# Expert stage with a fifth bank of up products, one bank for both turns, and places split 10 x 128 + 1

## The reference

```python
E, K = (8, 2); capacity = int(1.25 * N * K / E) + 1      # N = 4096, so 1281
k_probs, k_idx = top_k(softmax(xf @ router_w.T), K)       # shares normalised
rank = position of the token among those of its expert; keep = rank < capacity
buf = zeros((E, capacity, H)).at[flat_e, slot].add(where(keep, xf[token_id], 0))
h = silu(einsum('ech,ehf->ecf', buf, w1))                 # H = 128, F = 512
out_buf = einsum('ecf,efh->ech', h, w2)
combined = sum over k of out_buf[flat_e, slot] * keep * k_probs
return combined + x
```

## Time and profile before

| | |
|---|---|
| median of 3 runs | 1129.29 us (1127.92 to 1129.47) |
| profiled execution, its own time | 1126.79 us |
| its span | 1125.0 us |
| TensorE busy | 993.5 us, 88% |
| VectorE busy | 832.7 us, 74% |
| ScalarE busy | 775.5 us, 69% |
| GpSimd busy | 644.6 us, 57% |
| mean granted clock of TensorE | 0.968 |

### The profile page before, as it was taken

One profiled execution on the slowest core, in us unless ns is written; L12 is line 12 of the kernel. 1 busy time (PEld: TensorE's weight loads), 2 busy tenths in 40 slices (PEclk: granted clock), 3 DMA queues, 4 the chain that ended last, 5 costly groups with the idle time before them and its releaser, 6 DMA issues. The chain is left out here.

```text
span 1125.0 us, 18399 instructions
## 1 busy us (share of the span) xinstructions
PE 993.5 (88%) x5064; PEld 426.3 (38%) x5064; DVE 832.7 (74%) x1591; ACT 775.5 (69%) x1524; POOL 644.6 (57%) x781
## 2 busy tenths in 40 slices
PE   4699999998999999869999999999999977888860
PEld 3123333333333332213344444444444354544430
DVE  4588888897888888748777767777777664565555
ACT  1067777776777777647788888888888666676651
POOL 6444545362636333336669787787878640655565
PEclk9999999999999999979999999999999998999995
DMA  2553836041314131369977886877887327112136
GB/s 58 97 89 102 186 98 131 21 81 42 59 28 71 43 48 46 105 184 272 228 206 200 236 231 182 237 208 198 227 226 205 87 89 246 54 57 78 28 99 241
DMA packets 102378, 149.78 MB, mean 133 GB/s; under 512 B 18216, under 2 KB 72088, under 8 KB 101838
## 3 DMA queue, kind: packets, MB, share of 16 engines
q1 hardware_dynamic: 95470, 139.65, 47.2%
q0 software_dynamic: 6272, 8.94, 2.8%
q10 hardware_dynamic: 544, 0.13, 0.2%
HBM read 109.44 MB, written 40.04 MB: 133 GB/s over the span
## 5 line engine op out<-in xcount | busy, mean ns | idle before, releaser
L811 ACT ACTIVATE a_probs<-a_score 128x512 f32<-128x512 f32 x512 | 291.9, 598 | 119.0 <-PE a_score L892 112.0
L987 DVE TENSOR_REDUCE a_mx<-a_mxps 128x2 f32<-128x1024 f32 x256 | 306.6, 1211 | 51.3 <-PE a_mxps L883 46.5
L1585 POOL TENSOR_TENSOR m_hidl<-m_hid,m_hidh 128x512 f16<-128x512 f32 x203 | 234.4, 1168 | 74.4 <-ACT m_hidh L1648 67.0
L1654 ACT ACTIVATE m_h<-m_h 128x512 f32<-128x512 f32 (+1 forms) x264 | 153.7, 583 | 48.7 <-PE m_h L1772 42.6
L1868 DVE TENSOR_TENSOR m_hid<-m_h,p_gates 128x512 f32<-128x512 f32 x196 | 134.0, 688 | 65.2 <-ACT m_h L1654 58.7
L904 PE MATMUL a_ops<-a_probs,a_vst 128*32 128x512 f32 x1024 | 138.1, 612 | 0.0
L1648 ACT ACTIVATE m_hidh<-m_hid 128x512 f16<-128x512 f32 x203 | 126.2, 622 | 11.0 <-DVE m_hid L1868 10.5
L1750 PE MATMUL m_y<-m_hidh,p_wdh 128*128 128x512 f16 (+1 forms) x264 | 100.3, 380 | 9.9 <-POOL m_hidl L1585 7.8
L2154 POOL DMA_INDIRECT t_picked<-e_yrow,p_rows x66 | 65.8, 998 | 75.2 <-DVE e_yrow L2289 55.6
L892 PE MATMUL a_score<-a_qstack,a_kstack 128*128 128x512 f16 x256 | 97.6, 387 | 6.7 <-ACT a_probs L811 3.5
L2302 DVE SCALAR_TENSOR_TENSOR e_hidl<-e_h,e_hidh 128x468 f16<-128x468 f32 (+1 forms) x96 | 57.5, 603 | 60.6 <-ACT e_hidh L2170 47.6
(11 more groups left out here) (308 smaller groups left out, 1933.1 us busy)
## 6 DMA issues: line engine op xcount, KB each, us to landing
p_gates<-t_cw SPq DMA_DIRECT2D x256, 256.0 KB
t_slots<-p_blank SPq DMA_DIRECT2D x8, 723.9 KB
t_qparts<-a_qparts SPq DMA_DIRECT2D x32, 128.0 KB
t_picked<-p_blank SPq DMA_DIRECT2D x8, 512.0 KB
p_raw<-up SPq DMA_DIRECT2D x8, 512.0 KB, 4.9
p_raw<-down SPq DMA_DIRECT2D x8, 512.0 KB, 5.1
p_rows<-t_slots SPq DMA_DIRECT2D x5, 723.9 KB
a_xin<-x SPq DMA_DIRECT2D x8, 256.0 KB, 5.0
```

Of the source, the lines that this page charges most:

```text
L811: act.activation(probs[:, kt % 2, g, :], score[:, g % 2, :], ACT.Exp, scale=SCALE / (QS * QS)).then_inc(exp_done, 1)
L987: dve.tensor_reduce(mx[ahead % 2][:, j // 2, g:g + 2], mxps[:, j % 2, :, :], AX.X, ALU.max).then_inc(mx_done, 1)
L1585: pool.tensor_tensor(hidl[0:r0, k % r, :], hid[0:r0, k % r, :], hidh[0:r0, k % r, :], ALU.subtract).then_inc(lo_done[0], 1)
L1654: act.activation(h, h, ACT.Silu, scale=1.0 / WS).then_inc(silu_done, 1)
```

## The change

An expert now has exactly 1281 places: MAIN = 10 x 128 in ten full tiles, and one odd place. The blocks are 4, 4 and 2 tiles; the third has one column more for the odd place: 512, 512 and 257 columns. The odd records of experts 0 to 6 are loaded together by three small DMAs (rows, shares, targets), that of expert 7 with a blank one beside it by two more; all five are issued right behind the load of expert 1. The odd result of an expert is kept as one column, and all seven are turned, scaled and scattered together with expert 6, that of expert 7 with its own.

XBANKS and XLAG go from 4 to 5. The bank for it comes from the two turns: `xps` and `ops` are now the same bank `turned`. Hence new waits: turning the rows of block B waits for the result rows of block B - 4, and turning the result of B waits for `xl_done` of B + 4 (at most all). result_out is done at f = 0 of the second block after instead of f = 3 of the next; result_turned and result_rows at f = 2 instead of f = 1; split_weights at f = 1 instead of f = 2.

```diff
-CT = 11
-CR = -(-CAPACITY // CT)
-PLACES = CT * CR
+CT = 10
+CR = P
+PLACES = CAPACITY
+MAIN = CT * CR
@@ load_places, behind the load of an expert
+    if e == ODD_WITH:
+        odd_places(sp, scratch, pre)
+ODD_LOADS, ODD_WITH = 5, 1
+def odd_places(sp, scratch, pre):
...
+    for dst, src in ((pre.odd_rows[:], odd[0:E1 - 1, 0:D]), (pre.odd_share[:], diagonal(D)), (pre.odd_to[:], diagonal(D + E1)),
+                     (pre.odd_last[0:1, :], odd[E1 - 1:E1, :]), (pre.odd_last[1:2, :], pre.blank[1:2, :])):
+        sp.dma_start(dst, src, allow_slow_non_contiguous=True).then_inc(pre.x_in[ODD_WITH], 16)
@@ blanks_out
+                    sp.dma_start(odd, pre.blank[0:E1, :]).then_inc(pre.blank_out, 16)
@@ expert phase
-BLOCKS = ((0, 4), (4, 4), (8, 3))
+BLOCKS = ((0, 4), (4, 4), (8, 2))
-XLAG = 4
-XBANKS = 4
+XLAG = 5
+XBANKS = 5
-        xps, ops = ps("x", [P, 512]), ps("o", [P, 512])
+        turned = ps("x", [P, 512])
+        xps, ops = turned, turned
+        def copied(B):
+            return B + 1 + (B + 1) // NB
+        def rowed(B):
+            return B + 1 + (B >= ALL - 1 - NB) + (B >= ALL - 1)
+        def ends(B):
+            return at(B)[1] == NB - 1 and at(B)[0] >= E1 - 2
@@ GpSimd, behind the scatters of a block
+                if ends(B):
+                    last = e == E1 - 1
...
+                    pool.indirect_dma_start(plane, bass.IndirectOffsetOnAxis(to, 0), (odd_yrow_last if last else odd_yrow)[:], None,
@@ ScalarE, result_out
+                if at(B)[1] == NB - 1:
...
+                    act.activation(one, here, ACT.Copy).then_inc(yc_done, 1)
@@ ScalarE, main loop
-                if f == 3 and B:
-                    result_out(B - 1)
+                if f == 0 and B >= 2:
+                    result_out(B - 2)
             high_part(FC * ALL - 1)
+            result_out(ALL - 2)
             result_out(ALL - 1)
@@ TensorE, rows_turned
                 if B:
                     pe.wait_ge(xl_done, B)
+                if B >= 4:
+                    pe.wait_ge(row_done, rowed(B - 4))
...
+                        op = pe.matmul(xps[:, far:far + 1], pre.odd_rows[:], ident[0:E1 - 1, e:e + 1], start=True, stop=True)
@@ TensorE, result_turned
-                pe.wait_ge(yc_done, B + 1)
+                pe.wait_ge(yc_done, copied(B))
+                pe.wait_ge(xl_done, min(B + 4, ALL))
                 if B:
-                    pe.wait_ge(row_done, B)
+                    pe.wait_ge(row_done, rowed(B - 1))
@@ TensorE, main loop
-                if f == 1 and B >= 2:
+                if f == 2 and B >= 2:
                     result_turned(B - 2)
-            result_turned(ALL - 2)
             for g in range(FC * ALL - XLAG, FC * ALL):
                 down(g)
+                if g == FC * ALL - XLAG + 2:
+                    result_turned(ALL - 2)
@@ VectorE, result_rows and main loop
+                if ends(B):
...
+                        dve.tensor_scalar(odd_yrow[:], ops[0:E1 - 1, far:far + P], pre.odd_share[:], None, ALU.mult
+                                          ).then_inc(row_done, 1)
-                if f == 2 and B in SPLIT_IN:
+                if f == 1 and B in SPLIT_IN:
                     split_weights(dve, pre, JOBS + 1 + SPLIT_IN[B])
-                if f == 1 and B >= 2:
+                if f == 2 and B >= 2:
                     result_rows(B - 2)
```

More of the change, by code:

```diff
@@ L157, in place_buffers, with odd @@
         self.rows_in = [ctx.enter_context(nc.sbuf_tensor(f"p_rows{k}", [CR, CT, REC], F32)) for k in range(XEARLY)]
+        def odd(n, p, w, dt=F32):
+            return ctx.enter_context(nc.sbuf_tensor("p_odd_" + n, [p, w], dt))
+        self.odd_rows, self.odd_share, self.odd_to = odd("rows", E1 - 1, D), odd("share", E1 - 1, 1), odd("to", E1 - 1, 1)
+        self.odd_last = odd("last", 2, REC)
         self.x_in = [ctx.enter_context(nc.semaphore(f"p_x_in{k}")) for k in range(XBUFS)]
@@ L491, in blanks_out @@
                     sp.wait_ge(pre.blank_ready, 2)
-                into = scratch["slots"][PLACES * k:PLACES * k + PLACES, :].rearrange("(p t) c -> p t c", t=CT)
+                    odd = scratch["slots"].rearrange("(e p) c -> e p c", p=PLACES)[:, MAIN, :]
+                    sp.dma_start(odd, pre.blank[0:E1, :]).then_inc(pre.blank_out, 16)
+                into = scratch["slots"][PLACES * k:PLACES * k + MAIN, :].rearrange("(p t) c -> p t c", t=CT)
                 sp.dma_start(into, pre.blank[0:CR, :].unsqueeze(1).broadcast_to([CR, CT, REC])).then_inc(pre.blank_out, 16)
@@ L2106, in cols @@
         def cols(B):
-            return slice(0, CR * at(B)[3])
+            return slice(0, CR * at(B)[3] + (at(B)[1] == NB - 1))
         def put_by(b, experts):
-            return 16 * BLOCKS[b][1] * experts
+            odd = (experts > E1 - 2) + (experts > E1 - 1) if b == NB - 1 else 0
+            return 16 * (BLOCKS[b][1] * experts + odd)
+        def copied(B):
[4 more added lines that the diff above has]
+            return at(B)[1] == NB - 1 and at(B)[0] >= E1 - 2
         def pieces(t):
@@ L2149, in _ @@
                 e, b, t0, nt = at(B)
-                pool.wait_ge(row_done, B + 1)
+                pool.wait_ge(row_done, rowed(B))
                 for t in range(nt):
@@ L2181, in result_out @@
                     act.wait_ge(o_full, B - 1)
+                if at(B)[1] == NB - 1:
+                    e, far = at(B)[0], CR * at(B)[3]
+                    one, here = odd_y[:, min(e, E1 - 2):min(e, E1 - 2) + 1], yps[:, B % 2, far:far + 1]
+                    if e == E1 - 1:
+                        one, here = odd_y_last[:], here.broadcast_to([P, 2])
+                    act.activation(one, here, ACT.Copy).then_inc(yc_done, 1)
                 act.activation(yT[B % 2][:, cols(B)], yps[:, B % 2, cols(B)], ACT.Copy).then_inc(yc_done, 1)
@@ L2282, in result_rows @@
                 rows = rows_in[e % XBUFS]
+                if ends(B):
+                    far = P * nt
+                    if e == E1 - 1:
+                        dve.scalar_tensor_tensor(odd_yrow_last[:], ops[0:2, far:far + P], pre.odd_last[:, D + e:D + e + 1],
+                                                 pre.odd_last[:, 0:D], ALU.mult, ALU.add).then_inc(row_done, 1)
+                    else:
+                        dve.tensor_scalar(odd_yrow[:], ops[0:E1 - 1, far:far + P], pre.odd_share[:], None, ALU.mult
+                                          ).then_inc(row_done, 1)
                 if e == E1 - 1:
```

27 lines of the change are left out of this document (23 added, 4 removed).

## The result

The changed kernel took 1152.28 us (median of 4 runs, 1148.91 to 1153.21), the kernel before beside it 1129.11: ratio 1.0202 [1.0181, 1.0223], 2.0% slower, +23.2 us. The forecast was 1142 with a range of 1124 to 1163; the measured time lies outside the 1134 to 1150 that the forecast itself covered, and next to the 1153 of rival 2. The profiled execution took 1148.91 us for a span of 1147.2 (before: 1126.79 and 1125.0).

The account below looks back on a forecast made before the run. The end was bound by expert 6's late result rows, 14 scatters and a tail, with TensorE idle 22.1 us behind ScalarE's holds. -25.4 + 35.1 + 1.0 + 1.4 = +12.1 on 1126.79, plus 2.5 for the median: 1142 us, range 1124 to 1163.

Parts of the forecast that it names:

- the forecast itself: The case that the changed kernel takes 1134 to 1150 us; chance 0.50.
- rival 2: Waits at block starts lower TensorE's clock: 1153 us if the seven longest do it, 1165 if most do; chance 0.13.
- The shared bank: TensorE waits for result rows at the starts of blocks 3 to 22, 1.25, 2.3 or 1.7 us each: +35.1 us.
- split_weights at f=1: Weight splitting on VectorE, moved to step 1: the same instructions beside the same cover, 0.
- ScalarE's holds: Expert stage: runs of eight scatters hold ScalarE up; they no longer form, so idle time and slow clock go, -25.4 us.
- The clock: Three half-speed stretches of TensorE in the expert stage cost 4.8 us, which go; counted within the -25.4.
- TensorE's work: Expert products over 1281 instead of 1287 columns, -0.5 us; turns plus odd column nothing within 0.3; taken as 0 in all.
- The fifth bank: Up products wait for the low half five units back, not four: 1.3 us more patience against ScalarE's holds within a block.
- The start: Five small loads on the sync queue delay the stores that the expert stage's start awaits: +1.0 us, ends 0 and 2.1.
- The tail: After the last products, still 14 scatters; GpSimd ends 13.1 us behind TensorE instead of 11.7: +1.4 us.
- The signs of a wrong forecast: TensorE's idle time ahead of the turns under 20 us in all, or ScalarE's gaps persisting with runs of four scatters.

Follow-up runs that it names:

- experiment 1: The best version: the changed kernel with a bank for each of the two turns and four up banks, without the shared bank's waits; 1105.15 us, 0.9791 to the kernel before.
- experiment 2: The changed kernel with VectorE's result rows of step 2 issued ahead of its wait for the high half; 1125.07 us, 0.9972 to the kernel before.
- Experiment 7: The changed kernel with the weights split at step 3 of the block instead of step 1; 1151.02 us, 1.0235 to the kernel before.
- experiment 8: The kernel before with the scatters of experts 0 to 6 replaced by one-column memsets, those results missing from the output; 1097.86 us, 0.9762 to the kernel before.
- experiment 4: The kernel before with only the 10 tiles of 128 rows and the odd places; banks, lag and order as before; 1122.83 us, 0.9959 to the kernel before.
- experiment 5: The kernel before, 11 tiles of 117 rows, with only the change's lag of 5 and later steps; 1123.49 us, 0.9987 to the kernel before.
- experiment 10: The kernel of experiment 1 with the weights split at step 3 instead of 1, on a second chip; 1115.09 us, 0.9922 to the kernel before.
- experiment 9: The kernel before with two GpSimd additions between the scatters of blocks 0 and 1 in experts 0 to 6, on the second chip; 1137.84 us, 1.0146.
- experiment 11: The kernel of experiment 10 with one GpSimd addition between the scatters of blocks 0 and 1 of experts 0 to 6, on a third chip; 1100.49 us, 1.0016.
- experiment 3: The changed kernel with 6, 16 or 10 unread products of 257 columns ahead of each block-start wait; 1143.2 us, 1.0123 to the kernel before.
- experiment 6: The changed kernel with four up banks instead of five, the shared bank kept and one bank unused; 1150.92 us, 1.0226 to the kernel before.
- experiment 12: The kernel of experiment 1 with one GpSimd addition between the scatters of blocks 0 and 1, on the third chip; 1100.0 us, 1.0011 to the kernel before.

## Why the prediction was right, and where it was off

It was right in sign and in both mechanisms: the stops go, the shared bank costs more. In size it was 10 to 11 us low (+12.1 forecast; +22.1 in the profiled execution, +23.2 in the medians), mostly by the clock, which belongs to rival 2.

- *The shared bank, +35.1.* Forecast 1.25, 2.3 and 1.7 us in 20 places; measured 1.26, 2.34 and 1.68 in 17 of 20 places, 38.4 in all. The excess is the three blocks with a split, at 2.97, 2.63 and 2.62 instead of 1.68. Experiments 1 and 2 show the chain behind it. That the sizes agree to 0.04 us is partly luck: from the last up product's end to the rows' end it takes 2.52 us at block 1 (2.46 worked out), but then 0.15 us pass until the turn starts (1054.27 to 1054.42), which the working left out, and the down group ends 0.16 us later behind the product than it had (1051.75 to 1052.07), which takes that off again.
- *split_weights at f=1, 0.* This step failed: the same instructions no longer have the same cover, as at f=1 they stand ahead of lo(f2) and the rows, on the chain that the change had just made the bound. +3.2. VectorE's timeline ahead of the wait of 2.97 us (TensorE's turn starts at 967.59) has the second half of a split, then the low half, then the rows:
```profile
965.29 1.22 DVE L245 SCALAR_TENSOR_TENSOR p_wdl<-p_raw,p_wdh 128x1024 f16<-128x1024 f32 x1
966.43 0.68 DVE L2378 SCALAR_TENSOR_TENSOR e_hidl<-e_h,e_hidh 128x512 f16<-128x512 f32 x1
967.03 0.41 DVE L2365 TENSOR_TENSOR e_yrow<-e_x,p_rows 128x256 f32<-128x256 f32 x1
```
  Experiment 7 adds that the other place tried, step 3, isn't free either.
- *ScalarE's holds, -25.4.* TensorE's other idle time fell by 19.8 (22.05 to 2.3), forecast 20.6. The cause was an inference from coincidence; experiment 8 confirmed it, with 27.3 us of the stage and 26.6 of the whole, the clock's part in them. That length is what matters is supported by experiments 1, 4, 5 and 10, in which six to eleven scatters close together mostly go with a stop and fours mostly parted by 1.15 us or more do not; none of these runs changes the length alone. It is not the whole rule: the last stop of experiment 1 begins four scatters into its run (the product for it ended at 1067.04) and is over at 1071.45, with seven more scatters to come, and not 1.3 us past the run's end as the prediction had it. A direct test failed (9) or fell on a chip without stops (11).
- *The clock, -4.8.* This term was mis-sized: rival 2, which I gave 0.13, came true beside the forecast. Instead of nothing, 8.6 us are lost at the low level, +3.8 over before where I had -4.8. Rival 2 put it at +11 if the seven waits of 2.3 us each did it; the low level begins behind four of the seven, and once with the wait of 2.97 us (at 967.59). The other three waits of 2.34 us were followed by no fall, so the length of a single wait doesn't decide it. The Trainium skill ("TensorE: Matmul & The Clock Gate", "A second HAM failure mode: psum-queue depth-cycling") says that short idle pieces between groups of matmuls, if frequent enough, make the clock swing between its two levels. The traces agree: the change has 20 such pieces and five low stretches behind the stage's first microseconds, and experiment 3, in which the pieces are filled and so shortened, holds a clock of 1.00 from 940 to 1100.
- *TensorE's work, 0.* 3.2 us more, of which most is this: each odd column is a matmul in two passes of its own (14 for experts 0 to 6, from 938.7 to 1076.3) and delays TensorE by 0.31 us an expert, 2.4 in all; "nothing within 0.3" was said of what comes eight times.
- *The fifth bank* was costed at 1.3 us of patience; experiment 6 shows it worth nothing here, since what it would ride out is gone or greater.
- *The start, +1.0.* The sync queue's timeline, which answers to the earlier trace rows, has the five loads where I put them, 1.9 us in all, but between the first store of t_s (918.96) and the stage's first turn (931.25) 12.29 us pass, 12.91 before: -0.6. *The tail, +1.4:* 0.9.
```profile
920.89 0.34 SPq L200 DMA_DIRECT2D p_odd_rows<-t_slots  x1
...
922.22 0.59 SPq L200 DMA_DIRECT2D p_odd_last<-p_blank  x1
923.86 0.39 SPq L1574 DMA_DIRECT2D t_s<-m_srow  x1
```

In the profiled execution: 25.7 (stage: idle 18.7, clock 3.8, work 3.2) - 0.6 + 0.9 - 0.9 (behind GpSimd's end) - 3.1 (stages ahead, where the kernels are alike, and which differ so much from run to run) = 22.0 of 22.1. The sizes of the last two are differences that these two executions show, and are not explained. The signs of a wrong forecast that I had named (idle ahead of the turns under 20 us, stops with runs of four) did not come.

What stays open is why ScalarE stops, and why only on some chips. For one that has no stops, the change should cost the shared bank in full: from 1.0202/0.9791 = 1.042 and the 1.0011 of experiment 12, about 4.3%, an estimate that no run tried.

## What to carry to other kernels

A buffer shared by two users puts the slower user's whole chain on the path at each turn; work the chain out instruction by instruction from a clean stretch (here it came to within 0.04 us) and then ask of every other moved call whether it now stands on that chain. TensorE's idle pieces of 2.3 us, repeated, cost it clock too, here behind four of seven: price them with it. Before a gain is ascribed to a schedule, look whether the stalls that it removes exist on every chip: here nothing of the best version's 2.1% was left on the chip that has none (1.0011, with one addition between the scatters).

## What the runs showed of the hardware

- On the first two chips ScalarE stands still, mostly for 2.5 to 4.5 us, though its input is ready, late in or just behind a run of GpSimd's indirect DMAs, one every 1.28 to 1.30 us. Removing the scatters removes it (0.9762). Runs of eight with 117 rows each and with 128 (experiment 4) both have it. In the last run of the stage it can be longer: in experiment 9 the last down product ended at 1093.89 and ScalarE's copy of it began at 1101.04, with scatters going on from 1086.04 to 1109.83.
- It is a matter of the chip: on the third one the same instructions at the same pace stop ScalarE in neither of the two traces, and the kernel before takes 1099.0 us instead of 1123 to 1129.
- Work added to TensorE's waits made the kernel faster by 9 us (experiment 3), its granted clock then being 1.00 from 940 to 1100.
- Less waiting for VectorE made the best version slower by 1.3% (experiment 10, on another chip than experiment 1): its trace has GpSimd's runs joined, and four stops of ScalarE in the middle of the stage where experiment 1 had none.
